# Attention kernel on one core: ten sets of query chunks instead of eight groups of four, and reciprocal rows spread by DMA

## The reference

```
h = group_norm(x) * gn_w + gn_b
q, k, v = qw@h + qb, kw@h + kb, vw@h + vb
attn = softmax(q^T k / sqrt(128), axis=-1)      # 1024 x 1024 per image
out = x + pw @ (v @ attn^T) + pb
```

## Time and profile before

| What | Value |
|---|---|
| Time, median of 3 runs | 144.86 us (143.2, 144.86, 144.88) |
| The profiled execution | 144.58 us |
| Its span, first to last instruction | 142.6 us |
| PE busy | 132.4 us, 93% of the span |
| DVE busy | 98.9 us, 69% |
| ACT busy | 67.0 us, 47% |
| POOL busy | 26.7 us, 19% |
| Mean granted TensorE clock | 0.987 of full speed |
| `pT<-blocks` DMAs | 112, of 128 KB each |

### The profile page before, as it was taken

The page is one execution under the profiler, slowest core; times in us unless marked ns, Lnnn a source line. Parts: engine busy times, 40 slices in busy tenths (PEclk is TensorE's granted clock), DMA queues, the critical chain, the costliest instruction groups (busy, mean ns, idle before and its releaser), DMA issues.

```text
span 142.6 us, 2008 instructions
## 1 busy us (share of the span) xinstructions
PE 132.4 (93%) x666; PEld 112.9 (79%) x666; DVE 98.9 (69%) x169; ACT 67.0 (47%) x111; POOL 26.7 (19%) x33
## 2 busy tenths in 40 slices
PE   5998986758999999999999999999999999999990
PEld 5996863536888888888888888888888888888880
DVE  0587899999267968889887876977677865711122
ACT  4053759674045666364454574644433464330300
POOL 5053050840001036011002351030003000300300
PEclk9999999996899999999999999999999999999999
DMA  4950000299519960998069936894499667991031
GB/s 139 304 219 0 0 0 5 45 209 208 129 41 206 213 136 0 202 202 184 0 152 205 203 107 147 201 206 113 95 203 205 163 130 164 206 273 41 0 110 37
DMA packets 8073, 19.26 MB, mean 135 GB/s; under 512 B 2176, under 2 KB 2944, under 8 KB 8064
## 3 DMA queue, kind: packets, MB, share of 16 engines
q1 hardware_dynamic: 7376, 18.88, 55.7%
q10 hardware_dynamic: 688, 0.27, 0.7%
HBM read 2.36 MB, written 2.10 MB: 31 GB/s over the span
## 4 chain that ended last, share of the span: by engine, by line
PE 84%; DVE 5%; issue 4%; SPq 3%; DMA 2%; POOL 0%; DVEq 0%; POOLq 0%
PE ACC L290 35%; PE S L254 9%; PE S L255 8%; PE S L258 8%; PE S L199 5%; PE A L234 4%; SPq L139 3%; DVE blocks L561 3%; PE A L306 2%; PE S L315 2%; PE ACC L315 2%; DMA pT<-blocks 2%; PE A L272 2%; DVE s_sb L552 1%; PE A L212 1%
## 5 line engine op out<-in xcount | busy, mean ns | idle before, releaser
L552 DVE TENSOR_SCALAR_CACHE_REDUCE s_sb<-S,row_term 128x1024 f32<-128x1024 f32 x32 | 40.9, 1279 | 21.9 <-PE S L258 21.9
L290 PE MATMUL ACC<-pT,v 128*128 128x256 f32 x224 | 54.4, 389 | 0.7 <-DMA pT<-blocks 0.7
L290 PEld LDWEIGHTS ACC<-pT,v 128*128 128x128 f32 x224 | 42.3, 195 | 6.4 <-ACT v L399 0.9
L407 ACT ACTIVATE s_sb<-s_sb,rowmin 128x1024 f32<-128x1024 f32 x32 | 36.8, 1150 | 17.5 <-DVE s_sb L552 17.5
L561 DVE STREAM_TRANSPOSE blocks<-s_sb 128x1024 f32<-128x1024 f32 x28 | 34.7, 1240 | 0.0
L254 PE MATMUL S<-h_hi,g_hi 128*128 128x512 f32 x64 | 30.4, 475 | 2.5 <-DVE s_sb L552 1.9
L255 PE MATMUL S<-h_lo,g_hi 128*128 128x512 f32 x64 | 25.1, 393 | 0.0
L258 PE MATMUL S<-h_hi,g_lo 128*128 128x512 f32 x64 | 19.9, 392 | 0.0
L685 POOL TENSOR_TENSOR xb<-rden_bc,xb 128x512 f32<-128x512 f32 x7 | 8.9, 1275 | 57.3 <-DVE rden_bc L574 57.3
L254 PEld LDWEIGHTS S<-h_hi,g_hi 128*128 128x128 f32 x64 | 12.1, 189 | 5.9 <-DVE s_sb L552 2.4
L399 ACT COPY v<-A 128x384 f32<-128x384 f32 (+1 forms) x12 | 5.3, 443 | 20.3 <-PE A L234 20.3
(11 more groups left out here) (86 smaller groups left out, 109.4 us busy)
## 6 DMA issues: line engine op xcount, KB each, us to landing
pT<-blocks SPq DMA_DIRECT2D x112, 128.0 KB, 2.4
out<-xb SPq DMA_DIRECT2D x7, 256.0 KB, 2.7
x_sb<-x SPq DMA_DIRECT2D x1, 1024.0 KB, 6.9
x_sb<-x SPq DMA_DIRECT2D x2, 256.0 KB, 3.1
x_sb<-x SPq DMA_DIRECT2D x1, 512.0 KB, 3.7
w_in<-weights ACTq DMA_DIRECT2D x2, 128.0 KB, 3.6
out<-xb SPq DMA_DIRECT2D x2, 128.0 KB, 1.9
cols<-vectors ACTq DMA_DIRECT2D x1, 3.0 KB, 2.9
```

The lines of the kernel that those rows point to most:

```text
L290: last = pe.matmul(to, v[:, b % 3, t, :], pT[:, g % 2, 2 * pair:2 * pair + 2, t, :], start=(t == 0), stop=(t == KT - 1))
L407: act.activation(s_sb[:, c % 3, :], s_sb[:, c % 3, :], ACT.Exp, bias=rowmin[:, c % CH:c % CH + 1], scale=-1.0, accum_out=den[:, g % 2, k:k ...
L552: dve.tensor_scalar(s_sb[:, c % 3, :], S[:, c % 2, :], row_term[:, b % 2, i:i + 1], None, ALU.add, ALU.min, accum_out=rowmin[:, i:i + 1]). ...
```

## The change

The 32 chunks are cut into ten sets, of 2, 2, 4, 4, 4, 4, 4, 4, 2 and 2 chunks. Sets 0 and 9 are transposed by PE and copied through `pair_T`, which is now one buffer for both. Sets 1 and 8 are moved by DMA like the sets of four, with 16 DMAs each, of 32 rows of 2048 bytes; their two units take all 32-column parts at once and one half of the keys each, so the first of them waits for all four `moved` semaphores. Units 0 to 3 are issued at steps 3, 5, 7 and 9 rather than 7 to 10, unit m from 4 on at step m + 7 as before.

For sets 0 to 7 the reciprocals take another path: PE turns the columns of a set in one instruction into 2 or 4 rows (`turn_rden`), ACT copies these to `rden_rows` (`copy_rows`), SP stores them in DRAM (`row_store`), waits for that store, and loads them back with each row repeated on 128 partitions (`spread_rows`). Sets 8 and 9 keep the PE broadcast, into `S`. Some waits and PSUM places follow from this: the two transposes of set 0 go to `ACC`, and wait until DVE has read g of image 0 (`g_lo_ready`), `project_g(0, 1)` goes to `A1`. Ahead of the loop two DVE statistics instructions move behind `split_first_g`.

```diff
+SETS = (2, 2, 4, 4, 4, 4, 4, 4, 2, 2)
+
+FIRST_UNIT_STEPS = (3, 5, 7, 9)
...
+            def move_set(n):
+                sp.wait_ge(blocks_ready, FIRST[n + 1] - SETS[0])
+                if n > 2:
+                    sp.wait_ge(part_done, FIRST[n - 1])
...
+                        sp.dma_start(moved_view(n)[Q * j:Q * (j + 1), a].rearrange("p t n -> p (t n)"),
+                                     blocks_view(n)[Q * a:Q * (a + 1), j].rearrange("p t c q -> p (t c q)"))\
+                          .then_inc(moved[n % 2][a], 16)
+
+            def spread_rows(n):
+                sp.wait_ge(rows_ready, n + 1)
+                sp.dma_start(row_store[n, 0:P * SETS[n]].rearrange("(c q) -> c q", q=P), rden_rows[0:SETS[n], n % 2, :])\
+                  .then_inc(rows_stored, 16)
+                sp.wait_ge(rows_stored, 16 * (n + 1))
+                if n > 1:
+                    sp.wait_ge(out_ready, n - 1)
+                sp.dma_start(rden_bc[:, n % 2, 0:P * SETS[n]], row_store[n:n + 1, 0:P * SETS[n]].to_broadcast([P, P * SETS[n]]))\
+                  .then_inc(rows_spread[n % 2], 16)
...
+            spread_rows(0)
+            move_set(1)
+            spread_rows(1)
+            store_set(0)
+            for n in range(2, LS - 1):
+                move_set(n)
+                if n > 2:
+                    store_set(n - 2)
+                spread_rows(n)
+            move_set(LS - 1)
+            for n in range(LS - 3, NS):
+                store_set(n)
...
+            def turn_rden(n):
+                b = FIRST[n + 1] // CH if n > 1 else 0
+                pe.wait_ge(rden_ready, n + 1)
+                pe.wait_ge(v_ready, VP * (b + 1))
+                pe.wait_ge(row_ready, VP * (b + 1))
+                if n > 0:
+                    pe.wait_ge(rows_ready, n)
+                pe.transpose(A1[0:SETS[n], 0:P], rden[:, n % 2, 0:SETS[n]], ident[:, :]).then_inc(rows_psum, 1)
...
+            def moved_unit(n, u):
+                b, size = FIRST[n] // CH, SETS[n]
+                a0, width, half = (2 * (u // 2), 2, u % 2) if size == GC else (0, NQ, u)
...
+                    for a in range(a0, a0 + width):
+                        pe.wait_ge(moved[n % 2][a], MOVED * ((n + 1) // 2))
+                to = sums[n].rearrange("p (a n) -> p a n", a=NQ)[:, a0:a0 + width]
+                for t in range(PT * half, PT * (half + 1)):
+                    last = pe.matmul(to, v[:, b % 3, t, :], moved_view(n)[:, a0:a0 + width, t, :], start=(t == 0), stop=(t == KT - 1))
...
             def transpose_probs(c):
...
+                    to = (ACC[:, f, :] if c < SETS[0] else (A1, A0)[f])
+                    if c == 0:
+                        pe.wait_ge(g_lo_ready, HALVES)
...
                     value_tiles(b, 2)
-                    if b > 0:
-                        broadcast_rden(2 * b - 1)
+                if i == 3 and (b == 0 or c > CH):
+                    turn_rden(2 * b if b > 0 else 0)
+                if i == 5:
+                    turn_rden(2 * b + 1)
                 if i == 6 and b < L:
                     project_g(b + 1, 0)
-                    broadcast_rden(2 * b)
                 if i == 7 and b < L:
                     value_tiles(b + 1, 0)
-                if c > DIRECT:
+                if c > 0 and is_direct(c - 1):
                     transpose_probs(c - 1)
-                if LAG <= c < UNITS + LAG:
-                    value_part(c - LAG)
-            value_part(STEPS - LAG)
+                if c in FIRST_UNIT_STEPS:
+                    value_unit(FIRST_UNIT_STEPS.index(c))
+                if c >= LAG + GC:
+                    value_unit(c - LAG)
+            value_unit(STEPS - LAG)
             transpose_probs(STEPS - 1)
-            for m in range(STEPS - LAG + 1, UNITS):
-                value_part(m)
-            broadcast_rden(NG - 2)
-            broadcast_rden(NG - 1)
-            value_pair(0)
-            value_pair(1)
+            for m in range(STEPS - LAG + 1, FIRST[LS - 1]):
+                value_unit(m)
...
+            def copy_rows(n):
+                act.wait_ge(rows_psum, n + 1)
+                if n > 1:
+                    act.wait_ge(rows_stored, 16 * (n - 1))
+                act.copy(rden_rows[0:SETS[n], n % 2, :], A1[0:SETS[n], 0:P]).then_inc(rows_ready, 1)
...
+                if i == 4:
+                    copy_rows(2 * b if b > 0 else 0)
+                if i == 6:
+                    copy_rows(2 * b + 1)
...
-            half_stats(1, 1)
-            channel_stats(1)
             dve.wait_ge(wpv_ready, 1)
             split_first_g()
+            half_stats(1, 1)
             split_g(0, 0)
+            channel_stats(1)```

Here `FIRST[n]` is the first chunk of set n, NS is 10, LS is 9, and `is_direct(c)` holds for chunks 0, 1, 30 and 31.

SP at the start of the loop, before (`pT` is the moved transpose, `xb` the output):

```order
L153 DMA x_sb<-x 128x2x1024
L139 DMA pT<-blocks 32x1024 [waits blocks_ready]
L139 DMA pT<-blocks 32x1024 x15
L139 DMA pT<-blocks 32x1024 [waits blocks_ready]
L139 DMA pT<-blocks 32x1024 x15
```

More of the change, by code:

```diff
@@ L34, in build @@
     L = B - 1
[L35 to L38, removed]
+    NS = len(SETS)
+    LS = NS - 1
+    FIRST = [sum(SETS[:k]) for k in range(NS)]
+    DIRECT = FIRST[LS]
+    SPREAD_BY_DMA = NS - 2
     UW = 2 * CQ
@@ L52, in sem, with set_of, is_direct, direct_number @@
             return ctx.enter_context(nc.semaphore(name))
+        def set_of(c):
+            n = max(k for k in range(NS) if FIRST[k] <= c)
+            return n, c - FIRST[n]
+        def is_direct(c):
+            return c < SETS[0] or c >= DIRECT
+        def direct_number(c):
+            return c if c < SETS[0] else c - DIRECT + SETS[0]
+        def columns(n):
+            b, i = FIRST[n] // CH, FIRST[n] % CH
+            return b, slice(P * i, P * (i + SETS[n]))
+        def divided_in(c):
+            for n in range(1, NS):
+                last = FIRST[n] - 1
+                if c == (FIRST_UNIT_STEPS[last] + (2 if n == 1 else 1) if last < GC else last + LAG + 1):
+                    return n - 1
+            return None
         w_in = sb("w_in", [P, 4, P])
@@ new lines, in broadcast_rden, with direct_unit @@
+            def broadcast_rden(n):
+                pe.wait_ge(rden_ready, n + 1)
+                pe.wait_ge(rowmin_ready, STEPS - 1)
+                for c in range(SETS[n]):
+                    last = pe.transpose(S[:, 0, BANK * (n % 2) + P * c:BANK * (n % 2) + P * (c + 1)],
+                                        rden[:, n % 2, c:c + 1].to_broadcast([P, P]), ident[:, :])
+                last.then_inc(bc_psum, 1)
+            def direct_unit(n, half):
+                if half == 0:
+                    for f in range(HALVES):
+                        pe.wait_ge(pair_ready[f], 2 if n == 0 else 4)
+                    pe.wait_ge(v_ready, VP if n == 0 else VP * B)
+                    if n == 0:
+                        pe.wait_ge(gvar_ready, 2)
+                for t in range(PT * half, PT * (half + 1)):
+                    last = pe.matmul(sums[n], v[:, FIRST[n] // CH % 3, t, :], pair_T[:, t].rearrange("p d q -> p (d q)"),
+                                     start=(t == 0), stop=(t == KT - 1))
+                last.then_inc(part_done, 1)
@@ L287, in value_part @@
[L287 to L290, removed]
-                last.then_inc(part_done, 1)
+                    if n > 2:
+                        pe.wait_ge(normed_ready, n - 1)
+                    else:
+                        for f in range(HALVES):
+                            pe.wait_ge(pair_ready[f], 2)
@@ L555, in transpose_blocks @@
             def transpose_blocks(c):
[L556 removed]
+                n, k = set_of(c)
                 dve.wait_ge(probs_ready, c + 1)
[L558 removed]
+                if n > 2 and k == 0:
                     for a in range(NQ):
[L560 to L561 removed]
+                        dve.wait_ge(moved[n % 2][a], MOVED * ((n - 1) // 2))
```

273 lines of the change are left out of this document (124 added, 149 removed).

## The result

The changed kernel takes 160.51 us (median of 4 runs, 159.77 to 161.19) against 144.08 us before in the same series: a ratio of 1.114, 95% interval 1.104 to 1.124. Its profiled execution took 160.29 us, with a span of 158.3. The stretch ahead of the first matmuls of scores(0) differs by up to 4 us between the traces (they start at 11.6 to 15.8 us), so where two traces are compared I count from the start of scores(0) to the end of the last matmul. That is 127.30 us before (139.33 - 12.03) and 142.73 after (155.09 - 12.36).

The account below looks back on a forecast made before the run. PE was taken as the bound, with SP's queue second. Front 8.0, units -3.2, broadcasts -1.8, two waits 0.8, middle 0.6 and end 10.0 sum to +14.4 on 144.58: 159.0 us, range 149.5 to 162.5.

Parts of the forecast that it names:

- case A: DMA issue time goes by kind of transfer, not bytes, 0.636 us a move; 155 to 162 us, 62 in 100.
- The price of a small move: SP's queue: a move of 32 rows of 2048 bytes, absent from the trace, taken to cost 0.636 us to issue.
- the two bounds: Issue of a small move on SP: 0.636 us from the 4096-byte move, or 0.33 + 0.04 from DRAM transfers.
- The landing of 2.1: A small move lands in 2.1 us, between smaller stores' 1.9 and the larger moves' 2.4.
- The front: Up to set 1's first unit: its moves land at 41.6, PE idles 5.3 us, delay +8.0.
- Between: From set 1's first unit to the end of scores(27): gains of 3.2 and 1.8, losses of 0.8 and 0.6.
- -3.2 - 1.8 + 0.8 + 0.6: Two units already done; cheaper turns for broadcasts; waits at project_g(1, 1) and unit 4; SP's late moves.
- The two units and the turns: PE work saved: two units done early, -3.2; single turns replacing broadcasts of groups 1 to 5, -1.8.
- The end: After scores(27) end (t0): set 8 lands at t0 + 32.4, PE idles 10.5 us, lower clock 1.5; +10.0.
- Rival B: Small moves go by their bytes, 0.37 us each, saving 3.9 us at front and end: 151.2; 24 in 100.
- Rival C: SP becomes the bound throughout, each of six sets costing 0.6 us more: 162.6; 8 in 100.
- Rival D: The filled front pays if trips and small moves are quick: front -3.8, end -0.4, 140.4 us; 6 in 100.

Follow-up runs that it names:

- e4: The changed kernel with the 16 moves of set 8 cut into 32 DMAs for the same bytes: 171.73 us, ratio 1.183.
- e2: The changed kernel with 8 of the 16 moves of set 8 issued by ACT instead of SP: 155.80 us, ratio 1.071.
- e1: The changed kernel with SP issuing set 8's moves right behind set 7's, ahead of set 5's store and set 7's row transfers: 158.41 us, ratio 1.086.
- e5: The changed kernel with chunks 28 and 29 transposed by PE again, without set 8's move: 150.96 us, ratio 1.046.
- e3: The changed kernel with the first unit of set 1 at step 8 instead of 7: 154.54 us, ratio 1.065.
- e10: The changed kernel with 18 extra DMAs of six kinds in SP's idle start, to measure issue prices: 163.25 us, one run, time not meaningful.
- e6: The changed kernel with the row transfers (store, wait, load) on POOL's queue instead of SP's: 158.47 us, ratio 1.099.
- e8: The changed kernel with chunks 28 and 29 transposed by PE again and set 1's first unit at step 8: 145.33 us, ratio 1.006.
- e9: e8 with chunk 0 and 1 transposes a step later, unit 0 at step 4, set 1's reciprocals turned at step 6: 142.46 us, ratio 0.993.

## Why the prediction was right, and where it was off

The forecast was 159.0 us by case A, and the profiled execution took 160.29. Case A's mechanism is shown, not only argued: e4 and e2 change the number of issues in both directions and the time follows with 0.6 to 0.7 us for each; e1 moves them and the wait follows; e5 and e3 take away one wait each, and 9.6 and 6.0 us of the 16.4 go.

- **The price of a small move.** Taken as 0.636 from the nearest row; it is 0.591 and 0.04 between two. The choice between the two bounds was right, and its reason holds for moves: neither bytes nor rows count (e4, e10). It was not safe where it was drawn from, a load and a store of different size: among stores alone 1024 bytes a row cost 0.33 and 2048 cost 0.58. The landing of 2.1 is 2.0.
- **The front.** Set 1 landed for 41.66; forecast 41.6. That the place is hit so closely is luck. The forecast had SP's row trip hold the moves, until 30.0. In the trace the blocks of chunk 3 held them: they were ready at 29.70, not 28.9, and SP at 29.4, since the trip was shorter (1.14 us from store to load, not 2.3). e6 bears this out: without the trip on SP the moves began no sooner. And scores(0) started at 12.36, not at 12.03 - 0.4: the 0.4 is there (they come 1.93 us behind the first matmul of `project_g`, and came 2.27 behind it before), but this execution reached `project_g` 0.7 us later. The +8.0 is +8.03 by the span; from scores(0) it is +7.7 (29.30 against 21.60), where the forecast's own times give +8.4. PE was idle for 4.29 instead of 5.3 us, since it arrived 1.1 us later than counted.
- **Between.** From that unit to t0 I had -3.6 against before (-3.2 - 1.8 + 0.8 + 0.6), and the trace gives 72.24 (41.66 to 113.90) against 74.90, -2.7. The two units and the turns gave 3.0 and 1.6, not 3.2 and 1.8. The waits came to 1.63 us, not 1.4, and not where I had put them: 0.46 at `project_g` and 0.15 at set 2, nothing for a late SP (trips took 1.1 to 2.1 us, and the loads 0.33 to issue, not 0.6), but 1.02 at a step that I had priced as pure gain, where `turn_rden(2)` stands in A1 and waits for row terms from DVE. Small things make up the other 0.3.
- **The end.** Set 8 landed for t0 + 31.5, forecast 32.4: SP began set 7 with its blocks, at t0 + 5.9 and not 6.4, the trip took 2.0 and not 2.3, the load 0.33 and not 0.6. PE came at t0 + 22.9, not 21.9, and was idle for 8.6 us, not 10.5. 0.71 of that delay is a wait ahead of set 7's second half, which I had left out: the two PE transposes that stood ahead of it are gone. It costs nothing here, since PE waits for set 8 behind it. The clock was under-priced: PE lost 2.6 us to it, not the 1.5 of the earlier trace rows. This is the term that was most mis-sized, and the length of the wait does not explain it, as the last section shows. Sum: 41.19 us from t0, forecast 40.8; +10.4 for +10.0.

From scores(0) the three parts are +7.7, -2.7 and +10.4, together the 15.4 by which 142.73 exceeds 127.30. The forecast's +14.4 is by the time of the executions, where +15.7 was measured (160.29 - 144.58).

- **Rival B** fell with the first row of the issues (0.59 for 64 KB), and by e4, e2 and e10. The sentence of the Trainium skill that it could lean on ("DMA: Bandwidth & Descriptors", section "Issuing engines are not separate DMA queues") says that several issuing engines save only the time to initiate, which is usually small. Here, e2 shows that time to be the bound: half the issues on a second queue gave 4.7 us.
- **Rival C** did not happen: SP needed 13.9 us (105.42 to 119.27) for a set of four.
- **Rival D** asked what a filled front pays once nothing waits. It had -3.8 there; e8, with both waits gone and the front's units early, is 0.7 us longer than before from scores(0). Two more PE transposes (1.7) eat most of the 2.2 that the turns save on PE, and PE still waits, since set 1 is not there when PE arrives: its waits behind scores(0) sum to 7.0 us in e8, against 4.8 before and 1.5 for the lower clock. Only e9, where they sum to 4.0, gets below.

## What to carry to other kernels

Count DMAs, not bytes, where one queue issues them: cutting a group of chunks in two leaves it 16 issues, so the half group is ready hardly sooner (here 12 us from its blocks to its last landing), and it pushes everything behind it on that queue. Before filling an idle stretch of PE, write down what each new instruction waits for and what stands behind it, in order; two new waits of 1.5 and 1.2 us helped to undo the gain here, and moving the calls by a step took them out. A wait on PE costs its length and, often, the clock behind it. Before comparing two traces or two kernels by 1%, look at the granted clock of each execution: here the executions of the kernel before at 1.000 and at 0.988 are at least 1.0 us apart.

## What the runs showed of the hardware

- On SP's queue, a DMA from SBUF to SBUF costs 0.59 to 0.60 us to issue in the median (0.48 to 0.52 as the first after a wait), with 32, 64 or 128 rows and 512 to 4096 bytes a row (e10, e4). Loads from DRAM and small stores cost 0.26 to 0.44; stores of 128 rows of 2048 bytes cost 0.58 in a stream. I had not expected the ends to decide.
- A store of 1 to 2 KB to DRAM, with the wait for it, held SP for 1.1 to 2.1 us, and for 3.0 beside eight moves of ACT (e2).
- ACT and SP issue side by side: ACT's eight took 6.2 us, 0.8 each in a run of six (4.89), and SP's did not slow in the 2.4 us in which both issued moves.
- What the lower clock costs behind a stop does not grow with the stop. Ahead of the two units of set 8 (3.46 us at 2.4 GHz) waits of 4.60 (e2), 5.60 (e1), 6.22 (e6), 8.52 (e3), 8.63 (the change) and 18.32 us (e4) were followed by a loss of 3.1, 1.5, 2.8, 2.3, 2.6 and 2.8. In the front, waits of 4.29 (the change) and 4.31 (e5) cost 1.6 and 2.6, and before, stops of 1.72 and 0.70 cost 1.5. What sets the loss is open.
- Nor does one length of stop decide whether the clock falls. In the front of e3 and e8, with single waits of up to 1.5 us, it stayed at 2.4 GHz; in e1 it fell behind 1.03 and 0.76 us, one close behind the other. And of the executions of the kernel before some have a mean clock of 1.000 and some of 0.988 or less.
